# First cross-attention with its context rows on partitions: scores computed transposed, the maximum spread by a product, queries and results kept in DRAM

## What is computed

```python
# first stage; x is (8, 64, 512), context is (8, 1601, 384), 8 heads of 64
q = (layernorm(x) @ Wq).reshape(b, n, 8, 64)
k = (context @ Wk).reshape(b, m, 8, 64)
v = (context @ Wv).reshape(b, m, 8, 64)
sim = einsum('bihd,bjhd->bhij', q, k) * 64 ** -0.5
out = einsum('bhij,bjhd->bihd', softmax(sim, axis=-1), v).reshape(b, n, 512)
x = x + out @ Wout + bout
# then: self-attention, a mixture of experts, a second cross-attention with a long
# filter (s4d) and a feed-forward part, self-attention, a mixture of experts
```

## Time and profile before

| | us |
|---|---|
| median of 3 runs | 2034.78 (2028.33 to 2037.34) |
| the profiled execution | 2028.57 |
| its span, first to last instruction | 2026.7 |
| normalising, and the query products up to | 46 |
| attention, first scores to last weighting product | 50.8 to 551.5 |
| output of the stage, up to | 583 |
| PE busy in the span | 1834.5 (91%) |
| DVE, ACT, POOL busy in the span | 973.7, 558.5, 328.1 |
| mean granted TensorE clock | 0.921 of full speed |

### The profile page before, as it was taken

How to read it: one execution, slowest core, us unless ns; L and a number is a source line. 1 busy time by engine, 2 the same in 40 slices (tenths; PEclk the granted TensorE clock), 3 DMA queues, 4 the chain that set the end, 5 groups by cost and what they waited for, 6 DMA issues and landing times. The chain is left out here.

```text
span 2026.7 us, 24235 instructions
## 1 busy us (share of the span) xinstructions
PE 1834.5 (91%) x9264; PEld 1416.6 (70%) x9264; DVE 973.7 (48%) x1521; ACT 558.5 (28%) x949; POOL 328.1 (16%) x262
## 2 busy tenths in 40 slices
PE   6999999999978899688999879889789899999994
PEld 3899999999834777435677763277676567777772
DVE  1578686776713344439999713563436420000003
ACT  4354535445200111033434200043332221111110
POOL 1333123333000200223444200100000010000002
PEclk9899999999988899778999659989888799999997
DMA  3333131231142566451543130420200193374812
GB/s 118 98 98 98 49 98 51 96 99 59 36 167 101 185 235 232 128 197 49 203 147 110 49 110 31 181 84 0 85 0 1 50 368 143 136 278 182 316 60 68
DMA packets 109979, 243.11 MB, mean 120 GB/s; under 512 B 13824, under 2 KB 43024, under 8 KB 105248
## 3 DMA queue, kind: packets, MB, share of 16 engines
q1 hardware_dynamic: 100672, 220.97, 30.9%
q10 hardware_dynamic: 6624, 12.06, 1.7%
q0 software_dynamic: 2560, 8.39, 1.3%
HBM read 221.48 MB, written 19.92 MB: 119 GB/s over the span
## 5 line engine op out<-in xcount | busy, mean ns | idle before, releaser
L997 PEld LDWEIGHTS e_ps<-e_xg,e_w 128*128 128x128 f32 x2304 | 267.4, 192 | 43.3 <-issue 42.7
L997 PE MATMUL e_ps<-e_xg,e_w 128*128 128x128 f32 x2304 | 270.3, 276 | 4.5 <-issue 3.7
L370 PE MATMUL x_s_ps<-x_cxt,x_qs 128*128 128x400 f32 (+1 forms) x1152 | 245.9, 359 | 10.0 <-POOL x_qs L343 5.9
L396 PE MATMUL x_o_ps<-x_cx,x_pt 128*128 128x386 f32 (+1 forms) x1248 | 230.3, 343 | 0.0
L396 PEld LDWEIGHTS x_o_ps<-x_cx,x_pt 128*128 128x128 f32 (+1 forms) x1248 | 220.6, 190 | 1.4
L984 PE MATMUL e_ps<-e_w,xt 128*128 128x512 f32 x480 | 220.5, 599 | 0.3 <-DVE xt L1175 0.3
L370 PEld LDWEIGHTS x_s_ps<-x_cxt,x_qs 128*128 128x128 f32 x1152 | 207.0, 192 | 11.2 <-issue 11.1
L1152 DVE COPY e_y<-e_ps 128x512 f32<-128x512 f32 x24 | 16.5, 688 | 338.1 <-PE e_ps L984 338.1
L1890 PE MATMUL x_s_ps<-x_cxt,x_qs 128*128 128x512 f32 (+1 forms) x384 | 144.5, 534 | 9.4 <-POOL x_qs L2018 6.1
L984 PEld LDWEIGHTS e_ps<-e_w,xt 128*128 128x128 f32 x480 | 86.7, 192 | 83.1 <-issue 81.9
L1251 ACT ACTIVATE xt<-e_ps,e_b 128x128 f32<-128x128 f32 x192 | 54.7, 368 | 279.8 <-PE e_ps L997 279.8
(11 more groups left out here) (349 smaller groups left out, 2594.8 us busy)
## 6 DMA issues: line engine op xcount, KB each, us to landing
e_w<-in_L_ffn_W SPq DMA_DIRECT2D x16, 4096.0 KB, 18.8
x_cxt<-in_ctxT SPq DMA_DIRECT2D x8, 2401.5 KB, 9.8
x_cx<-in_ctx SPq DMA_DIRECT2D x8, 2304.0 KB
e_w<-in_L_ffn_gate_up_proj SPq DMA_DIRECT2D x8, 2048.0 KB, 9.1
x_stage<-in_ctxT SPq DMA_DIRECT2D x16, 768.0 KB, 4.3
x_stage<-in_ctx SPq DMA_DIRECT2D x16, 768.0 KB, 6.3
e_w<-in_L_ffn_down_proj SPq DMA_DIRECT2D x8, 1024.0 KB
ff_w<-in_L_xattn_W SPq DMA_DIRECT2D x2, 4096.0 KB, 12.5
```

What stands on the lines that cost most here:

```text
L370: last = nc.tensor.matmul(s_ps[:, n, 0:b - a], qs[:, u % 2, p, c, :], cxt[:, q, c, a:b], start=(m + c == 0), stop=(m + c == len(PARTS) + C ...
L396: last = nc.tensor.matmul(o_ps[:, 0:WIDE], pt[0:rows, p, t, :], cx[0:rows, q, t, :], start=(t + m == 0), stop=(t + m == KT - 1 + len(PARTS ...
L997: last = nc.tensor.matmul(u_ps[:, g % 2, a * PER + n, :], w1[:, e % PAIR, m, a * hidden + c * P:a * hidden + (c + 1) * P], xg[:, m, :], st ...
```

## The change

The stage becomes one block, and its unit becomes a step: one tile of up to 128 context rows of one batch element against all 512 query rows. There are 8 x 13 = 104 steps.

- **Scores** (`scores`, PE): 9 products of 512 columns with the context tile stationary and `qs` moving, so that scores come out with context rows on partitions. ACT copies them to a ring of 17 tiles `sc` in SBUF.
- **Maximum**: it must run over partitions and tiles. DVE keeps an elementwise running maximum `most` over the 13 tiles (one 128x512 instruction for a step), PE transposes it (4 tiles), DVE reduces it to `peak` and builds `diag`, and a product of ones with `diag` puts each query's maximum on all partitions (`spread_most`); ACT copies that to `nmax`.
- **Exponents**: 14 steps later POOL subtracts `nmax` from the tile (`lowered`), ACT takes the exponent and casts the high part to `pt`, DVE makes the low part, POOL adds the tile to `acc` for the sum. No transposes of exponents.
- **Weighting** (`give`, PE), 16 steps after the scores: 9 products of 512 columns, context tile stationary, `pt` moving, result 384 x 512 in three PSUM banks for all 13 steps of a batch element.
- **Sum**: a product of ones with `acc` gives the total; it goes to DRAM and comes back, and divides after the Wv products.
- **Queries** are written to DRAM (`asked`), and come back once per batch element (`ask`) in runs of 64 numbers; batch element 0 is split by POOL straight from the ring. **Results** are written to DRAM (`given`) and fetched at the end (`fetch`).
- **Context pieces** are half as large (128x768), 14 for a batch element; ACT still makes high parts, DVE the low parts of `cxt`, POOL those of `cx`.
- **Filter**: the same instructions, cut into 22 chunks per 128 channels, one chunk behind each step of DVE.
- The first context pieces, the weights and the filter's parameters are loaded during the normalisation.

```diff
-        with ExitStack() as c2:
-            EVEN = CTX + CTX % 2
-            WIDE = CD + 2
-            N_UNITS = B * H // 2
...
+    STEPS = B * KT
+    RAISE, GIVE = 14, 16
+    RING, SHIFT = 17, 15
...
+            @block.gpsimd
+            def _(pool):
...
+                for s in range(STEPS + GIVE):
+                    g = s - RAISE
+                    if 0 <= g < STEPS:
+                        rows = rows_of(g % KT)
+                        pool.wait_ge(nmax_ready, g // KT + 1)
+                        pool.wait_ge(copied, g + 1)
+                        G.tensor_tensor(place(g)[0:rows], place(g)[0:rows], nmax[0:rows], ALU.subtract).then_inc(lowered, 1)
+                    for p in pieces:
+                        if p.step == s and not p.turned:
+                            pool.wait_ge(ch_ready, p.count)
+                            G.tensor_tensor(part(p, 1), raw(p), part(p, 0).bitcast(F32), ALU.subtract).then_inc(cl_ready, 1)
+                    g = s - RAISE - 1
+                    if 0 <= g < STEPS:
+                        b, t = g // KT, g % KT
+                        rows = rows_of(t)
+                        pool.wait_ge(exp_ready, g + 1)
...
+                            G.tensor_tensor(acc[0:rows, b % 2, :], acc[0:rows, b % 2, :], place(g)[0:rows], ALU.add).then_inc(sum_ready, 1)
...
+            @block.tensor
+            def _(pe):
+                def scores(g):
+                    b, t = g // KT, g % KT
+                    if g >= 3:
+                        pe.wait_ge(copied, g - 2)
...
+                        for m, (a, q) in enumerate(PARTS):
+                            last = nc.tensor.matmul(ps[0:rows, S_BANK + g % 3, :], cxt[:, a, c, lo:lo + rows], qs[:, q, c, :],
+                                                    start=(c + m == 0), stop=(c + m == CC + 1))
+                    last.then_inc(s_ready, 1)
+
+                def give(g):
...
+                    pe.wait_ge(pt_ready, g + 1)
...
+                            last = nc.tensor.matmul(ps[:, O_BANK + c, :], cx[0:rows, a, t, c * P:(c + 1) * P], pt[0:rows, g % 3, q, :],
+                                                    start=(t + m == 0), stop=(t + m == KT + 1))
+                    last.then_inc(o_ready, 1)
...
+                for s in range(STEPS + GIVE):
+                    g = s - GIVE
+                    b, t = s // KT, s % KT
+                    if t == 0 and g >= 0:
+                        give(g)
+                    if s < STEPS:
+                        scores(s)
+                    if t == 0 and 1 <= b <= B:
+                        turn_most(b - 1)
+                    if t == 1 and 1 <= b <= B:
+                        spread_most(b - 1)
+                    if g >= 0 and g % KT == KT - 1:
+                        total(g // KT)
+                    if t and g >= 0:
+                        give(g)
...
+            @block.vector
+            def _(dve):
...
+                    if s < STEPS:
+                        rows = rows_of(t)
+                        dve.wait_ge(copied, s + 1)
...
+                            V.tensor_tensor(most[0:rows, :], most[0:rows, :], place(s)[0:rows], ALU.max).then_inc(most_ready, 1)
+                    for p in pieces[J:]:
+                        if p.step == s and p.turned:
+                            low_part(p)
+                    g = s - RAISE
+                    if 0 <= g < STEPS:
+                        rows = rows_of(g % KT)
+                        dve.wait_ge(hi_ready, g + 1)
+                        V.tensor_tensor(pt[0:rows, g % 3, 1, :], place(g)[0:rows], pt[0:rows, g % 3, 0, :].bitcast(F32),
+                                        ALU.subtract).then_inc(pt_ready, 1)
+                    filter_step(s + J - 1)
...
+            @block.scalar
+            def _(act):
...
+                    if s < STEPS:
+                        rows = rows_of(t)
+                        act.wait_ge(s_ready, s + 1)
...
+                        if s >= RING:
+                            act.wait_ge(pt_ready, s - RING + 1)
+                            act.wait_ge(sum_ready, s - RING + 1)
+                        A.copy(place(s)[0:rows], ps[0:rows, S_BANK + s % 3, :]).then_inc(copied, 1)
...
+                    if 0 <= g < STEPS:
+                        rows = rows_of(g % KT)
+                        act.wait_ge(lowered, g + 1)
+                        A.activation(place(g)[0:rows], place(g)[0:rows], ACT.Exp).then_inc(exp_ready, 1)
+                        act.wait_ge(exp_ready, g + 1)
+                        if g >= 3:
+                            act.wait_ge(o_ready, g - 2)
+                        A.copy(pt[0:rows, g % 3, 0, :], place(g)[0:rows]).then_inc(hi_ready, 1)
+                    for p in pieces[J:]:
+                        if p.step == s:
+                            high_part(act, p)
```

More of the change, by code:

```diff
@@ L1569 @@
     QUARTER = R // 4
+    CHUNKS = 22
     PI2_HI = 6.28125
@@ L1648, in angles @@
         self.sync(dve)
-        self.step(V.tensor_scalar(turns, ang, PI / 2, -2 * PI, ALU.is_gt, ALU.mult))
-        self.sync(dve)
-        self.step(V.scalar_tensor_tensor(turns, ang, PI / 2, turns, ALU.add, ALU.add))
-        self.sync(dve)
+        if half == 0:
+            self.step(V.tensor_scalar(turns, ang, PI / 2, -2 * PI, ALU.is_gt, ALU.mult))
+            self.sync(dve)
+            self.step(V.scalar_tensor_tensor(turns, ang, PI / 2, turns, ALU.add, ALU.add))
+            return
         self.step(V.tensor_scalar(ang, ang, self.TOP, -self.TOP, ALU.min, ALU.max))
@@ L1657, in powers @@
         V = self.core.nc.vector
-        pw, mag, sm = self.pw, self.mag, self.sm
-        are, aim, cre, cim = (self.par[:, n, i, :] for n in range(4))
+        pw, mag = self.pw, self.mag
         dve.wait_ge(self.powers_ready, i * 3 + 3)
@@ L1662, in powers, with ratios @@
             self.step(V.tensor_tensor(pw[:, a, :, :], pw[:, a, :, :], mag[:, :, :], ALU.mult))
+    def ratios(self, dve, i):
+        V = self.core.nc.vector
+        pw, sm = self.pw, self.sm
+        are, aim, cre, cim = (self.par[:, n, i, :] for n in range(4))
         self.sync(dve)
@@ L1692, in coefficients, with starts @@
         self.sync(dve)
-    def starts(self, dve):
+    def starts(self, dve, half):
         V, R, STEP = self.core.nc.vector, self.R, self.STEP
@@ L2543, in laid_out @@
         "numbers": np.tile(np.arange(1, P + 1, dtype=np.float32), (P, 1)),
+        "heads": np.kron(np.eye(8, dtype=np.float32), np.ones((1, S), np.float32)),
         "two_eyes": np.tile(np.eye(S, dtype=np.float32), (2, 1)),
```

836 lines of the change are left out of this document (439 added, 397 removed).

## The result

The changed kernel takes **2232.45 us** (2227.27 to 2235.8), the kernel before 2034.22 in the same comparison: ratio 1.0976 (1.0943 to 1.1009), 198 us more. The prediction said 2218, range 2120 to 2315. The profiled execution has a span of 2229.4 us against 2026.7; first scores to last weighting take 693 us (53.05 to 746.3) where they took 501.

What follows compares the result with a forecast made beforehand. PE bounds the old attention; afterwards DVE and POOL's shared SBUF time would. A bare 669 us plus 27, 16 and 25 of losses puts the last weighting at 737 against 551.5 (+186); tail +1 and half of 6 give 2218, range 2120 to 2315.

Steps and rivals of the forecast that it cites:

- PE's list shrinks, and does not set the pace: Attention: PE's products and transposes fall from 488 to 442 us, with PE idle for a third.
- Another of my signs: Steady part of the attention: the prediction is wrong if DVE or POOL idle for long there.
- Turns between DVE and POOL: Attention steps: instructions on SBUF exclude each other, so both lists add up, 6.11 us a step with filter; chance 0.83.
- The factor: DVE and POOL working on SBUF together take 0.887 of their summed lone times, from eight instructions of the old trace.
- The filter's share: Filter instructions on DVE beside the steps: 1.41 us of shared time a step, 142 in the sum.
- The bare sum: First scores to last weighting: 54 + 47 + 415 + 103 + 50 = 669 us, supposing DVE or POOL always has work.
- rival 2: Attention: short instructions do not exclude each other, the POOL and ACT chain sets 4.75 a step, about 2051 us; chance 0.04.
- Steps 14 to 81: Attention steps with the filter beside them: 68 x 6.11 = 415 us, plus 27 for the chain.
- Steps 82 to 103: Attention steps behind the filter: 22 x 4.70 = 103 us, plus 16 for the chain at 0.7 a step.
- Tail +1: After the last weighting: four inverse-sum products add 3.5 us, lost barriers save 2.5; the sum's DRAM trip stays hidden.
- Changes of batch element: Seven places in the attention where engines wait for transposes and the spread maximum: 3.5 us each, 25 in all.
- Rival 3: Attention: POOL and DVE overlap, slack hides the chain, PE sets the pace at 4.25 a step, about 2004 us; chance 0.05.

Runs made afterwards that it cites:

- experiment 3: The changed kernel with one product of three in scores and weighting, so PE does 6 products a step, not 18: 2200.29 us.
- probe 1: The kernel before with unused blocks of DVE and POOL additions ahead of its work: twelve each took 7.3 and 14.7 us alone, 20.15 at once.
- experiment 2: The changed kernel without the filter's instructions on DVE and ACT, the filter being a constant: 2106.84 us.
- experiment 12: The changed kernel with POOL's two-input instructions in its steps each replaced by three write-only fills of about the same length: 2110.96 us.
- experiment 7: The changed kernel with context pieces one step later, the running maximum read from PSUM, and PE making POOL's sum of exponents: 2146.21 us.
- experiments 5 and 6: The changed kernel with POOL taking each context piece one step later: 2224.61 us; the same with DVE's running maximum read from PSUM: 2197.76 us.

## Why the prediction was right, and where its steps were off

- **PE's list shrinks, and does not set the pace**: right. Product spacing is 230 ns, the 227 of the earlier trace rows; PE is busy for 76% of the main stretch where I said two thirds, and its mean granted clock was 0.88 there. I had written that I would be wrong if it fell below 0.9. It did, and experiment 3 shows that this was a poor sign: PE with a third of the products and at a clock of 0.60 changes 32 us. Another of my signs came true as well: POOL was idle for 134 of the 395 us, 105 of them in waits for ACT's cast.
- **Turns between DVE and POOL**: right that they cost, with L398 and L414 at 1.58 and 1.60 rather than the 1.7 I named, and L601 and L593 at 1.39 and 1.14, far over 0.69. The factor was 0.887 (0.889 by the eight durations listed, which add up to 8.62, not 8.64), measured 0.92 in probe 1. The filter's share (126 measured for 142 in the sum) fits in size, though 26 of it fell before step 14. The unit of my sum was wrong for single terms: 512 columns of DVE work with 0.61 us of shared time each gave 31 us in 96 instructions, not 59, and POOL's additions gave 62 of about 107. The bare sum supposed that one of the two always has work, with the chain as a small addition. The rows at 247 us read the other way round: the chain sets the pace, and turns lengthen it (no run tests this order by itself). The prediction had this too, as 12.5 us for two steps with a DVE turn before each of the five POOL instructions, and 12.8 was measured at 247 us.
- **How the loss divides, and luck**: my sum was 167 us above rival 2, which has no turns, and rival 2 some 20 above the kernel before. Measured, the turns cost 121 and the rest is about 80. The total of 2218 for 2232 owes something to luck: turns priced too high and the chain with its changes too low made up for each other.
- **The terms in time.** First scores at 53.05 (54). To POOL's first subtraction, at 115.2: 62 us for 47; without the filter, for which these steps had no room in my sum, it is 25 less (experiment 2). Steps 14 to 81, to the subtraction of step 82 at 565.27: 450 against 442 and five changes of 3.5, 460. Steps 82 to 103, to 687.1: 122 against 122, but made up differently: behind the filter the pair of 9.4 us sets the pace, which is rival 2's 4.75 a step and not 4.70 + 0.7, and long single waits such as the 9.4 us before 576.91 fill up the rest. Last steps to 746.3: 59 against 53; the chain holds for its three pieces too, which 3.15 a step left out. Each change of batch element is counted where it falls. Together 746.3 for 737: -1, +15, -9, -1, +6 (one from rounding); errors of both signs made the end fit better than its parts.
- **Tail +1**: 1483.1 us from the last weighting to the end, 1475.2 before (2026.7 less 551.5): +8. The sum's trip through DRAM was not hidden: PE waits 4.34 us for it up to 759.06, and then takes 6.20 us for the four products for which I had 3.5, at a mean granted clock of 0.57 from 759 to 766.
- **Changes of batch element**: the sum had 3.5 us each. In the changed kernel POOL's longest idle from step 14 on is at one of them (11.93 us before 368.52), partly waits that it would have had elsewhere; I can't separate them. In experiment 12 steps 14 to 103 took 465 us, 48 more than 90 times 4.63, and six changes fall there: an estimate from these numbers is 8 us each.
- **Ends of the range**: with the terms as the prediction names them the lower end is 2144, not 2140 (the tail's +1 and the 3 for the median were left out), and the upper about 2280, not 2285. The range holds either way.
- **Rival 2** (no turns) was to give 2051; experiment 12 is its world, and measured 2111. The pace was right (4.63 for 4.75), the start (first subtraction at 107.8 for 100), the changes and the last steps (52 for 43) were not. **Rival 3** needed PE's list to set the pace, at 4.1 a step. In the changed kernel it didn't, with or without the filter beside it; PE set the pace in experiment 7 alone, without POOL's additions and behind the filter, at 4.59 for its 20 products.

What stays open: why single removals give back from half (maximum, sum) to nine tenths (filter) of the shared time they take away. A reading that fits, and that no run tests, is that a DVE instruction costs only where it stands before one of POOL's five, and that with the filter's list behind it the next instruction takes the place of one that was removed. It is also untested what the chain costs by itself, since experiments 5 and 6 moved its waits and did not remove them.
